# Layer 2 of a four-layer gated cross-attention stack: weighing by whole batches, rounding on ScalarE, and a new order of the steps' parts on all engines

## The reference, cut to what matters

```python
# attention: 16 heads of 16 columns, keys and values from ctx_2048
scores = clip(q @ k.T / 4, -50, 50); masked rows -> -50
ctx    = softmax(scores) @ v
delta  = rs * (ctx @ Wo.T + bo)
delta  = (delta - mean) / sqrt(var + 1e-5) * gamma + beta
x      = x + tanh(g_xattn[2]) * delta
# feed-forward: 832 hidden columns, activations rounded to 8-bit steps, weights to -1, 0, 1
bitlinear(a, w) = act_quant(a) @ weight_quant(w).T
act_quant(a)    = clip(round(a * 127 / max|a|), -128, 127) / (127 / max|a|)
x      = x + tanh(g_ffn[2]) * bitlinear(silu(bitlinear(n, w_gate)) * bitlinear(n, w_up), w_down)   # n = layernorm(x)
```

## Time and profile before

| what | us |
|---|---|
| three executions | 1916.81, 1927.67, 1933.82; median 1927.67 |
| profiled execution, its own time | 1921.5 |
| its span (first to last instruction) | 1920.2 |
| granted TensorE clock over the span | 0.956 of full speed |

### The profile page before, as it was taken

One profiled execution on the slowest core, in us unless ns is written; L12 is line 12 of the kernel. 1 busy time (PEld: TensorE's weight loads), 2 busy tenths in 40 slices (PEclk: granted clock), 3 DMA queues, 4 the chain that ended last, 5 costly groups with the idle time before them and its releaser, 6 DMA issues.

```text
span 1920.2 us, 35897 instructions
## 1 busy us (share of the span) xinstructions
PE 1696.0 (88%) x12175; PEld 1177.6 (61%) x12205; DVE 1336.7 (70%) x4259; ACT 947.2 (49%) x2211; POOL 791.6 (41%) x957
## 2 busy tenths in 40 slices
PE   6989898979988999999796877778999999988998
PEld 2444444647756777777674554556777777766445
DVE  7888873624467888889647898864667667666447
ACT  2776674214424777777554555324444444443352
POOL 3333321176746656664625553220243333443350
PEclk7999999999997999999997999799999999999998
DMA  4454421139854443333214542028010000030857
GB/s 112 99 130 102 102 55 49 55 130 354 304 140 88 94 89 81 80 84 68 86 38 112 161 109 78 11 67 297 1 37 19 33 11 2 14 99 25 260 194 309
DMA packets 179669, 200.41 MB, mean 104 GB/s; under 512 B 85732, under 2 KB 149361, under 8 KB 176160
## 3 DMA queue, kind: packets, MB, share of 16 engines
q1 hardware_dynamic: 163456, 156.31, 29.9%
q0 software_dynamic: 15168, 41.54, 6.1%
q10 hardware_dynamic: 864, 0.26, 0.1%
HBM read 131.88 MB, written 75.44 MB: 108 GB/s over the span
## 4 chain that ended last, share of the span: by engine, by line
PE 53%; DVE 23%; ACT 8%; POOL 6%; issue 6%; DMA 2%; SPq 0%; DVEq 0%; ACTq 0%; POOLq 0%
PE psum L3400 3%; PE psum L3474 3%; DVE sbuf L539 3%; PE psum L389 3%; PE psum L1337 2%; PE psum L352 2%; PE psum L3449 2%; PE psum L1058 2%; PE psum L1702 2%; PE psum L3467 2%; PE psum L1356 2%; ACT sbuf L3837 2%; PE psum L2286 2%; PE psum L3436 2%; PE psum L1767 1%
## 5 line engine op out<-in xcount | busy, mean ns | idle before, releaser
L539 DVE TENSOR_REDUCE sbuf<-psum 128x2 f32<-128x512 f32 x256 | 164.4, 683 | 35.0 <-PE psum L352 34.0
L190 POOL TENSOR_TENSOR sbuf<-sbuf 128x1 f32<-128x1 f32 x128 | 73.4, 575 | 273.0 <-DVE sbuf L182 272.7
L2023 ACT ACTIVATE sbuf<-psum 128x512 f32<-128x512 f32 x256 | 137.4, 588 | 45.2 <-PE psum L1767 44.0
L3837 ACT ACTIVATE sbuf<-psum,sbuf 128x128 f32<-128x128 f32 x256 | 113.7, 455 | 88.8 <-DVE sbuf L3649 88.7
L678 ACT ACTIVATE sbuf<-psum 128x1024 f32<-128x1024 f32 x128 | 131.2, 1026 | 47.3 <-PE psum L374 43.0
L3929 POOL DMA_INDIRECT l_slot_inputs<-sbuf x96 | 97.1, 1011 | 100.0 <-DVE sbuf L3720 75.0
L3474 PE MATMUL psum<-sbuf 128*128 128x256 f32 x512 | 123.7, 385 | 4.9 <-DVE sbuf L3667 4.9
L352 PE MATMUL psum<-sbuf 112*128 112x256 bf16 x512 | 104.3, 288 | 15.8 <-DVE sbuf L539 11.1
L3400 PE MATMUL psum<-sbuf 128*128 128x256 f32 x512 | 115.8, 379 | 0.8 <-ACT sbuf L3801 0.8
L1892 DVE CUSTOM_DVE_ANT_0 sbuf<-psum,sbuf 128x128 f32<-128x128 f32 x512 | 112.5, 284 | 1.0 <-PE psum L1746 1.0
L3400 PEld LDWEIGHTS psum<-sbuf 128*128 128x128 f32 x512 | 96.1, 190 | 20.3 <-issue 8.6
(11 more groups left out here) (434 smaller groups left out, 4480.1 us busy)
## 6 DMA issues: line engine op xcount, KB each, us to landing
l_pair_outputs<-sbuf SPq DMA_DIRECT2D x24, 512.0 KB, 6.7
sbuf<-in_l_gu_pairs SPq DMA_DIRECT2D x32, 384.0 KB, 7.1
sbuf<-l_pair_outputs SPq DMA_DIRECT2D x16, 768.0 KB, 14.5
l_q_parts<-sbuf SPq DMA_DIRECT2D x32, 192.0 KB, 2.6
sbuf<-l_q_parts SPq DMA_DIRECT2D x16, 384.0 KB
sbuf<-l_q_parts SPq DMA_DIRECT2D x32, 192.0 KB
sbuf<-l_k_parts SPq DMA_DIRECT2D x32, 192.0 KB
sbuf<-in_l_down_pairs SPq DMA_DIRECT2D x32, 192.0 KB, 8.9
```

The costliest lines, as they stand in the source:

```text
L539: dve.tensor_reduce(top3[:, 2 * hp:2 * hp + 2, c], score_bank[v % 2].rearrange("p (j t) -> p j t", j=2), AXX, ALU.max, negate=True).then_i ...
L2023: act.activation(e_t[i % 4][:, h * BANK:(h + 1) * BANK], turn_bank[:, h * BANK:(h + 1) * BANK], ACT.Exp).then_inc(*exped.up())
L3837: last = act.activation(e_t[u % 3][:, j * P:(j + 1) * P], score_bank[:, j * P:(j + 1) * P], ACT.Exp, bias=mt[:, j:j + 1], scale=rq[:, lo + ...
```

## The change

- pe_weigh and dve_normalise take a whole batch: 32 small products into 512 columns of av_bank, one transpose of 128x512 instead of two of 128x256, one reciprocal, one multiply of 128x256, one transpose of 128x256. In step i both run for batch i - 1. The rows of Wo and bv are laid out to match. pe_project_out(i - 1) stands at the end of PE's step instead of the start of the next.
- The rounding of the hidden columns moves from DVE (L2936) to ACT: act_round_h(f), an Identity activation of 128x832 from SBUF to SBUF, behind a new wait on h_scaled; pe_turn_hq(f) and pool_out_scale(f) wait for it.
- The addition of epsilon to a variance moves from DVE to POOL, as an instruction of its own before each power (three places: pro_stats, delta, ffn_stats).
- The orders of all four engines change, as the diff shows.

```diff
+def ln_root_of_variance(m, n, var_ready, eps_added, rstd_ready, ring):
+    pool.wait_ge(*var_ready.at(n + 1))
+    pool.tensor_scalar(s[:, 8:9], s[:, 7:8], EPS_LN, None, ALU.add).then_inc(*eps_added.up())
+    pool.wait_ge(*eps_added.now())
+    pool.tensor_tensor(s[:, 8:9], s[:, 8:9], m.half_neg, ALU.pow).then_inc(*rstd_ready.up())
...
+    def pe_weigh(b):
+        pe.wait_ge(*clipped.at(2 * b + 2))
+        pe.wait_ge(*v_ready.at(b + 1))
+        if b:
             pe.wait_ge(*x_mid.at(b))
...
     def pe_project_out(b):
-        pe.wait_ge(*normed.at(2 * b + 2))
-        pe.wait_ge(*av_read.at(min(2 * b + 3, 2 * NB)))
+        pe.wait_ge(*normed.at(b + 1))
...
     def pe_program():
...
-            if y >= 0:
-                pe_project_out(y)
             if paired and i % 2 == 0:
                 pe_keys(i // 2 + 2)
             if paired and i % 2 == 1:
...
             pe_scores(2 * i + 1)
             if paired and i % 2 == 0:
                 pe_turn_x(i // 2 + 2)
+            if i % 2 == 1 and i + 2 < NB:
+                pe_values(i + 2)
             if f >= 0:
                 pe_turn_hq(f)
-            if i + 2 < NB:
-                pe_values(i + 2)
             if i:
-                pe_weigh(2 * i - 1)
+                pe_weigh(i - 1)
             if f >= 0:
                 pe_down(f)
-            pe_weigh(2 * i)
+            if i % 2 == 0 and i + 2 < NB:
+                pe_values(i + 2)
             if y >= 0:
                 pe_turn_xq(y)
             if i + 1 < NB:
                 pe_scores(2 * i + 2)
             if y >= 0:
                 pe_up(y)
-        pe_project_out(NB - 2)
+            if i:
+                pe_project_out(i - 1)
...
+        pe_weigh(NB - 1)
         ahead.pe_keys(0)
-        pe_weigh(2 * NB - 1)
+        pe_turn_xq(NB - 2)
         pe_down(NB - 3)
         pe_project_out(NB - 1)
-        pe_turn_xq(NB - 2)
         pe_up(NB - 2)
...
     def dve_ffn_gate(f):
...
-        dve.tensor_scalar(c(9), c(8), c(5), 127.0, ALU.mult, ALU.mult).then_inc(*chain.up())
-        dve.wait_ge(*chain.now())
-        dve.tensor_scalar(h, h, c(9), ROUND, ALU.mult, ALU.add).then_inc(*h_round.up())
+        dve.tensor_scalar(c(9), c(8), c(5), 127.0, ALU.mult, ALU.mult).then_inc(*h_scaled.up())
...
     def dve_program():
...
-            if i % 2 == 1:
-                dve_clip(2 * i)
             if f >= 0:
                 dve_ffn_gate(f)
             if y >= 0:
                 dve_delta_stats(y)
-            if i % 2 == 0:
-                dve_clip(2 * i)
+            dve_clip(2 * i)
             if y >= 0:
                 dve_add_attention(y)
                 dve_ffn_stats(y)
-            if i:
-                dve_normalise(2 * i - 1)
+            dve_clip(2 * i + 1)
             if y >= 0:
                 dve_ffn_quantise(y)
-            dve_clip(2 * i + 1)
-            dve_normalise(2 * i)
             if i % 2 == 1 and i // 2 + 3 < NPAIR:
                 dve_norm_stats(i // 2 + 3)
+            if i:
+                dve_normalise(i - 1)
...
+    def act_round_h(f):
+        act.wait_ge(*h_scaled.at(f + 1))
+        act.activation(h_t[f % 2], h_t[f % 2], ACT.Identity, bias=plus_round, scale=s_t[f % 3][:, 9:10]).then_inc(*h_round.up())
...
     def act_program():
...
             if j < 2 * NPAIR:
                 act_bias(j)
-                act_hi(j)
-            act_exp(2 * i + 1)
             if i % 2 == 0 and j < 2 * NPAIR:
                 act_keep_x(i // 2 + 2)
+            if i % 2 == 1 or f < 0 or j >= 2 * NPAIR:
+                act_exp(2 * i + 1)
+            if f >= 0:
+                act_round_h(f)
+            if i % 2 == 0 and f >= 0 and j < 2 * NPAIR:
+                act_exp(2 * i + 1)
+            if i % 2 == 1 and i + 2 < NB:
+                act_values(i + 2)
             if f >= 0:
                 act_keep_hq(f)
-            if i + 2 < NB:
-                act_values(i + 2)
             if y >= 0:
                 act_less_mean(y)
             if j < 2 * NPAIR:
-                act_mid(j)
+                act_hi(j)
             if f >= 0:
                 act_scale_out(f)
+            if i % 2 == 0 and i + 2 < NB:
+                act_values(i + 2)
             if y >= 0:
                 act_keep_xq(y)
+                act_tanh(y)
+            if j < 2 * NPAIR:
+                act_mid(j)
             if i + 1 < NB:
                 act_exp(2 * i + 2)
-            if y >= 0:
-                act_tanh(y)
         ahead.act_keep_x(0)
         ahead.act_square(0, 0)
+        act_round_h(NB - 3)
         act_keep_hq(NB - 3)
...
     def pool_program():
...
             if y >= 0:
                 pool_delta_root(y)
-            if j < 2 * NPAIR:
-                pool_rest(j)
             if f >= 0:
                 pool_out_scale(f)
             if y >= 0:
-                ln_root(m, y, f_var, f_rstd, ffn_stats)
+                ln_root_of_variance(m, y, f_var, eps_added, f_rstd, ffn_stats)
+                pool_scales(y)
+            if j < 2 * NPAIR:
+                pool_rest(j)
             if j < 2 * NPAIR:
                 pool_lo(j)
-            if y >= 0:
-                pool_scales(y)
             if f >= 0:
                 pool_add_out(f)
             if i % 2 == 1 and pair < NPAIR:
                 pool_roots(pair)
                 pool_norm(pair)
+            if i % 2 == 0 and i and pair < NPAIR:
                 for n in range(PAIR * pair, PAIR * pair + PAIR):
                     pool_add_beta(n)
```

More of the change, by code:

```diff
@@ L182, in ln_stats, with ln_stats_only @@
     dve.tensor_scalar(s[:, 8:9], s[:, 7:8], 1.0, EPS_LN, ALU.mult, ALU.add).then_inc(*var_ready.up())
+def ln_stats_only(m, src, n, var_ready, ring):
+    dve, chain, s = m.nc.vector, m.chain, ring[n % len(ring)]
+    dve.bn_stats(s[:, 0:6], src).then_inc(*chain.up())
+    dve.wait_ge(*chain.now())
+    dve.bn_aggr(s[:, 6:8], s[:, 0:6]).then_inc(*var_ready.up())
+def ln_root_of_variance(m, n, var_ready, eps_added, rstd_ready, ring):
+    pool, s = m.nc.gpsimd, ring[n % len(ring)]
+    pool.wait_ge(*var_ready.at(n + 1))
+    pool.tensor_scalar(s[:, 8:9], s[:, 7:8], EPS_LN, None, ALU.add).then_inc(*eps_added.up())
+    pool.wait_ge(*eps_added.now())
+    pool.tensor_tensor(s[:, 8:9], s[:, 8:9], m.half_neg, ALU.pow).then_inc(*rstd_ready.up())
 def ln_root(m, n, var_ready, rstd_ready, ring=None):
@@ L2552, in layer_2 @@
     part_t = [early.bf16(3 * KD * N) for _ in range(2)]
-    ones, minus_round = early.f32(P), early.f32(1)
+    ones, minus_round, plus_round = early.f32(P), early.f32(1), early.f32(1)
     stack = {"k": [early.bf16(H2 * S) for _ in range(2)]}
@@ L2557, in layer_2 @@
     d_t = [mem.f32(8 * P) for _ in range(4)]
-    turn_t = [mem.f32(D + P + 8) for _ in range(2)]
+    turn_t = mem.f32(2 * D + 2 * P + 16)
     v_t = [mem.f32(H2 * 32) for _ in range(4)]
@@ L2662, in pe_scores @@
         last.then_inc(*scored.up())
[L2664 to L2671, removed]
-            pe.wait_ge(*x_mid.at(b))
[L2673 to L2679, removed]
+    def pe_weigh(b):
+        pe.wait_ge(*clipped.at(2 * b + 2))
+        pe.wait_ge(*v_ready.at(b + 1))
+        if b:
+            pe.wait_ge(*x_mid.at(b))
+        v3 = split_cols(v_t[b % 4], H2)
+        for s in range(2):
+            d3 = split_cols(d_t[(2 * b + s) % 4], 8)
+            for j in range(2):
+                for q in range(4):
+                    at = (2 * s + j) * P
+                    last = pe.matmul(av_bank[32 * q:32 * q + 32, at:at + P], v3[:, 8 * s + 4 * j + q, :], d3[:, 4 * j + q, :],
+                                     start=True, stop=True, tile_position=(0, 32 * q))
         last.then_inc(*valued.up())
     def pe_project_out(b):
-        pe.wait_ge(*normed.at(2 * b + 2))
-        pe.wait_ge(*av_read.at(min(2 * b + 3, 2 * NB)))
+        pe.wait_ge(*normed.at(b + 1))
         if b == 0:
@@ L2807, in dve_set @@
         dve.memset(minus_round, -ROUND).then_inc(*set_ready.up())
+        dve.memset(plus_round, ROUND).then_inc(*set_ready.up())
     def dve_sum_weights():
@@ L3137, in act_program @@
         ahead.act_square(0, 1)
+        act_round_h(NB - 2)
         act_keep_hq(NB - 2)
@@ L3143, in act_program @@
         ahead.act_square(0, 3)
+        act_round_h(NB - 1)
         act_keep_hq(NB - 1)
@@ L3179, in pool_delta_root @@
     def pool_delta_root(b):
-        s = y_t[b % 2][:, 8:9]
+        s = y_t[b % 2]
         pool.wait_ge(*y_var.at(b + 1))
-        pool.tensor_tensor(s, s, m.half_neg, ALU.pow).then_inc(*y_rstd.up())
+        pool.tensor_scalar(s[:, 8:9], s[:, 7:8], EPS_LN, None, ALU.add).then_inc(*eps_added.up())
+        pool.wait_ge(*eps_added.now())
+        pool.tensor_tensor(s[:, 8:9], s[:, 8:9], m.half_neg, ALU.pow).then_inc(*y_rstd.up())
     def pool_scales(f):
@@ L3211, in pool_program @@
         for i in range(NB):
-            f, y, j, pair = i - 3, i - 2, made_in(i), i // 2 + 3
+            f, y, j, pair = i - 3, i - 2, made_in(i), (i - 1) // 2 + 3
             if y >= 0:
                 pool_delta_root(y)
```

(4 more changed lines are left out.)

47 lines of the change are left out of this document (22 added, 25 removed).

## The result

The changed kernel takes 1934.3 us (median of 20 executions, 1927.3 to 1938.9), the kernel before 1927.3 in the same comparison (20 executions). The ratio is 1.0034, 95% interval 1.0023 to 1.0046: slower by 0.34%, or 6.6 us (4.4 to 8.9; the two medians are 7.0 apart). The forecast was 1927.0, a sum of +2.4 us, in a range of 1905 to 1943. The range holds the result, and the change is one of "within 1%"; but 20 executions told 0.34% from nothing, and the loss is nearly three times the sum. The forecast's 1927.0 stands on four executions of the kernel before with a mean of 1924.9. Twenty have a median of 1927.3, so the number is by chance the time of the kernel before, and the sum of +2.4 is what the 6.6 has to be compared with.

A forecast was written before the change was run, and what follows sets the result against it. DVE was taken to fill a step before the change. Terms -4.6 - 1.5 + 10.7 + 1.6 - 6.3 + 2.5 = +2.4 us; forecast 1927, the mean 1924.9 and 2.1, range 1905 to 1943.

The forecast's parts named there:

- The even steps: Steps 4, 6, 8, 10: POOL's new order delays the pair's norm and the queues behind it, +10.7 us.
- the clock term: Even steps: a new PE idle may lower the clock and slow the transposes, 0.4 us four times, +1.6.
- the price of 14.2 for a step without the delay: Even steps: the length in us that the same chain gives without POOL's delay.
- Rival 1: POOL's delay is absent, even steps take 14.2; sum -9.2, 1918 us; chance 0.2.
- The odd steps and steps 12 to 15: Odd steps 5 to 11 bounded by ACT's chain, 13.3 us, -1.5; steps 12 to 15 take 52.4, -6.3.
- Rival 2: DVE stays the bound all through and ACT's chain keeps up; -26, 1901 us; chance 0.15.
- Rival 3: DVE stretches POOL's queue from lo to the norm, clock term at its upper end; +19, 1944 us; chance 0.15.
- The start: Steps 0 to 2, up to the end of the first quantising pass: 4.6 us earlier.
- step 3: Last step before the even and odd ones priced: stays at about 15.6 us, since its slow clock does.
- the 3.7 us by which the weights' rounding was to start earlier: Step 0: without the weighing there, the weights' rounding starts behind the clip, some 3.7 us earlier.
- The tail: After the loop: a gate 2.2 us later behind pe_project_out(15), and a little for each rounding left, +2.5.

The follow-up runs named there:

- e9: The changed kernel with e1's POOL order and e5's tail (old rounding and order); 1915.6 us against 1927.4 for before, ratio 0.9943.
- e1: The changed kernel with POOL's roots and norm of a pair ahead of pool_lo and pool_add_out; 1934.2 us against 1939.2 for before, ratio 0.9967.
- e2: The changed kernel with act_less_mean ahead of act_keep_hq on ACT in all steps; one execution of 1948.4 us.
- e3: The changed kernel with the rounding of batches 13, 14 and 15 back on DVE; one execution of 1947.9 us.
- e4: The changed kernel with the tail's old order on PE and DVE around project_out(15), rounding still on ACT; one execution of 1946.2 us.
- e5: The changed kernel with both tail edits, e3's rounding on DVE and e4's old order; one execution of 1941.7 us.
- e7: The kernel of e6 with e4's old tail order as well; 1937.3 us against 1940.2 for before, ratio 0.9970.
- e8: The kernel of e9 with act_less_mean ahead of act_keep_hq in odd paired steps; 1921.6 us against 1940.2 for before, ratio 0.9910.
- e6: The changed kernel with e1's POOL order and the rounding back on DVE in all steps and the tail; one execution of 1934.9 us.
- e10: The same kernel as e8, timed on another chip, beside e9; 1916.4 us against 1927.4 for before, ratio 0.9944.

## Why the prediction came out as it did

**The even steps: right in mechanism, 2.5 us short in size.** Stage by stage in step 6, as predicted and as measured from G: norm ends 6.85 / 6.65; turn of x 6.9 / 6.8; rounding ends 9.15 / 9.5, where the turn took 1.08 for the 0.65 assumed; keep_hq ends 11.5 / 12.5, since the seven transposes took 1.76 for 0.98; quantise ends 13.55 / 14.5; next gate 16.65 / 17.8. Steps 4 and 6, with a clock of 0.81, are 1.4 and 1.2 over 16.65, steps 8 and 10, at 0.90, 0.8 over, 4.2 us in all. In step 6, 0.9 of it is there at the end of the quantise, behind the slow turn and the slow transposes; the other 0.3 stands between the quantise and the gate, where PE is still at a later batch's values and starts turn_xq 0.45 after the quantise (0.06 at the end of step 9 in the kernel before). So the clock term, taken at 0.4 with bounds of 0 and 1.0 per step, belonged near its upper end. (The Trainium skill, "TensorE: Matmul & The Clock Gate", section "HAM oscillation — how this bites in real kernels", says that idle stretches send the clock back, and by it, the prediction said, this term would be at its upper end, +4. The trace agrees in these steps; e9's steps below show that it does not hold each time.) e1 confirms the cause, and its 13.9 shows that the price of 14.2 for a step without the delay was a little high. Rival 1 was wrong about the changed kernel and right about e1.

**The odd steps and steps 12 to 15: right.** Odd 13.2 against 13.3, with DVE idle 1.08 us for less_mean; 52.9 against 52.4. The rounding on ACT took 1.07 where 0.95 was taken (bounds 0.63 and 1.20), the transpose of 128x512 0.68 to 0.71 (0.7 taken), DVE 10.8 busy (under 11). Rival 2 needed ACT to keep up; the 1.08 us for which DVE waits show that it does not, and e2 shows the same by taking 0.6 of them away. Rival 3 needed a slow norm, and it took 2.57 in the steady steps; only at the start did it take 4.01, where DVE's weight rounding hid it.

**The start: not as firm as the ledger looks.** The ledger has -5.8 there and -2.0 in step 3. But e3, e4 and e5 have the changed kernel's code up to the tail, and their starts took 40.7 to 41.3 us, not 37.5. The first keys (eight products) say why. In the changed kernel's profile:

```profile
1015.51 1.97 PE L2634 MATMUL psum<-sbuf 128*128 128x256 f32 x8
```

In e5's profile, on another chip:

```profile
1032.92 3.76 PE L2634 MATMUL psum<-sbuf 128*128 128x256 f32 x8
```

And in the kernel before:

```profile
1016.14 3.37 PE L2617 MATMUL psum<-sbuf 128*128 128x256 f32 x8
```

The changed kernel's profile caught a start at the upper clock level and before's did not. Between starts at the lower level, the first scores to the end of step 3 took 58.9 before and 54.6 to 54.9 in e3 to e5: a gain of 4.0 to 4.3, near the 4.6 taken, and not 7.7. Its parts are other than predicted: the start itself gave 1.9 to 2.5 of the 4.6, and step 3, which was to stay, took 13.6 to 13.9 in these three. With POOL's norm first it took 13.1 and 12.6 in e7 and e8, at a clock of 0.99 and 1.00, and 14.9 to 16.4 in e1, e6, e9 and e10, at 0.84 and 0.85; e8 and e10 are one kernel, so this is the clock's doing and not the order's. What decides it was not settled. Of the twelve profiles here, two have the first keys at 1.97, the changed kernel's and e8's; in the others they took 3.4 to 3.8. With a gain of 4.1 in this stretch the terms add up to 11 us, where the comparison of 20 executions each gives 6.6 (4.4 to 8.9); what the other executions have that makes up the rest stays open. (The single executions of e3, e4 and e5, with what their tails gave back added, stand 10.9, 10.4 and 8.4 us above the medians beside them, so nearer to the 11; but twenty executions of one kernel spread over 12.) Two slips of working changed nothing: the 3.7 us by which the weights' rounding was to start earlier is 3.5 by its own terms, and the sum doesn't use it; and the forecast's 1927 is the mean and 2.1, for a sum of 2.4.

**The tail: the step that failed.** The prediction priced one late gate at 2.2 and said that "each of the roundings left adds a little", 0.3 together. The first interval did cost +2.2 (19.8 for 17.6). Its link to the gate is another than predicted: project_out(15) came late, at G + 14.4 for G + 11.9, but the gate of batch 14 didn't wait for the up product and its tanh, which had ended at 1258.66, 1.9 us before it; it waited for DVE's own work on batch 15, which stands behind project_out(15). That the size fits is in part luck.

The two intervals left cost +3.2 and +2.6. In the second the rounding brings the transposes only 0.4 later (G + 5.1 for G + 4.7). The rest is slow products behind PE's idle of 3.87 (2.89 before): transposes 1.76 for 0.98, the queries 4.98 for 3.62, two short groups between them 0.4 to 0.5 longer each, at a mean clock of 0.81 over the interval for 1.00. The rounding's engine alone doesn't decide that: with it back on DVE (e3) the interval still takes 17.7, again at 0.81; with only the order back (e4) 16.9, at 0.90; with both (e5) 15.2, at 1.00. In the third the transposes come 2.0 later, because the rounding stands behind act_square, and are slow as well. e3 takes all of the 2.6 away; e4, which keeps the wait but has the clock at 1.00 there, takes 1.6. So about 1.0 of it is the wait and 1.6 the clock. Over the whole tail e3 gives back 2.2, e4 3.4 and both together 7.0.

So the failed step is the size of this term: it priced a delay where it first strikes, and put the later intervals, and the lower clock behind longer idle stretches (0.90 over the tail, where it was 1.00), at next to nothing. The term is 5.4 over its estimate, more than the 4.2 between the sum and the measured 6.6; the next in size are the even steps, 2.5 over theirs. Which idle stretch lowers the clock, the second of the tail at 2.92 in e4 but not at 2.89 in the kernel before, stays open.

## What to carry to other kernels

When an operation moves to another engine, walk the queue that it joins at every place where the loop is unrolled by hand, the tail above all: the same rounding costs under 0.2 us in an odd step of the loop (e1 against e6) and up to 2.6 in one interval of the tail. When other engines' queues stand behind one producer (here POOL's normalisation of a pair, with PE's turn of x, ACT's rounding and POOL's own next root behind it), its place in its queue can cost more than the change saves on the engine that looks full: 14.8 us in the even steps, against 7.5 saved in the other steps from 5 to 15. And price an idle stretch of TensorE by the slow rows behind it, with the place where they fall: low clock in work that something covers is cheap, the same in work that the next step waits for is not.
